# Four-layer graph network on one core: the two input loads of a pair move from SyncE's queue to ScalarE's, and every engine's order of work is drawn again

## What is computed

```
h = relu(layernorm(x)); x = x + deg * (h @ Wi.T + b) + adj @ (h @ Wj.T)          # layer 0
h = relu(layernorm(x)); Wh = h @ W1
    x = x + softmax(mask(leaky(Wh @ a_src [:, None] + Wh @ a_dst [None, :]))) @ Wh  # layer 1
h = relu(layernorm(x)); H = h @ W2          # 128 columns
    x = x + concat(softmax(mask(leaky(H @ a0 [:, None] + H @ a1 [None, :]))) @ H, H)   # layer 2
h = relu(layernorm(x)); q, k, v = h @ Wq.T + bq, h @ Wk.T + bk, h @ Wv.T + bv
    x = x + concat(softmax(mask(q k.T / sqrt(32)), 8 heads) @ v) @ Wo.T + bo        # layer 3
```

## Time and profile before

| | us |
|---|---|
| median of 3 runs | 1317.21 (1314.80 to 1318.49) |
| the profiled execution | 1310.78 |
| its span, first to last instruction | 1309.0 |
| TensorE busy | 1240.0 |
| ScalarE busy | 1074.4 |
| VectorE busy | 1074.3 |
| GpSimd busy | 1011.2 |

### The profile page before, as it was taken

One profiled execution on the slowest core, in us unless ns is written; L12 is line 12 of the kernel. 1 busy time (PEld: TensorE's weight loads), 2 busy tenths in 40 slices (PEclk: granted clock), 3 DMA queues, 4 the chain that ended last, 5 costly groups with the idle time before them and its releaser, 6 DMA issues. The chain is left out here.

```text
span 1309.0 us, 43294 instructions
## 1 busy us (share of the span) xinstructions
PE 1240.0 (95%) x12013; PEld 1106.7 (85%) x12013; DVE 1074.3 (82%) x5137; ACT 1074.4 (82%) x3971; POOL 1011.2 (77%) x1600
## 2 busy tenths in 40 slices
PE   7899999999999999999999999999999999999997
PEld 5788888888888888888888888888888888889986
DVE  5798887888888888888788888888888888888874
ACT  3578888888888888888888888888888888888996
POOL 7778777788787787787787787887887787886763
PEclk9999999999999999999999999999999999999999
DMA  5323342344344434434432433433324434321000
GB/s 143 68 47 43 64 71 52 62 55 70 62 56 69 63 51 71 64 51 67 70 51 63 56 68 63 66 59 62 61 65 62 61 64 62 57 40 22 21 25 34
DMA packets 96523, 77.23 MB, mean 59 GB/s; under 512 B 31264, under 2 KB 88608, under 8 KB 96288
## 3 DMA queue, kind: packets, MB, share of 16 engines
q1 hardware_dynamic: 93808, 72.76, 33.1%
q10 hardware_dynamic: 2480, 1.71, 0.5%
HBM read 57.48 MB, written 16.95 MB: 57 GB/s over the span
## 5 line engine op out<-in xcount | busy, mean ns | idle before, releaser
L891 ACT ACTIVATE exps<-masked,nmax 128x128 f32<-128x128 f32 x1024 | 399.2, 404 | 0.0
L436 POOL TENSOR_TENSOR probs<-exps,rsum 128x512 f32<-128x512 f32 x256 | 266.1, 1040 | 17.7 <-DVE rsum L665 17.4
L657 DVE CUSTOM_DVE_ANT_0 masked<-bank,mask 128x128 f32<-128x128 f32 x1024 | 227.7, 284 | 8.0 <-PE bank L1113 4.3
L407 POOL TENSOR_SCALAR y<-x,nm,rstd 128x256 f32<-128x256 f32 x384 | 209.5, 556 | 11.9 <-issue 11.1
L891 ACT ACTIVATION_READ_ACCUMULATOR exps<-masked,nmax 128x1 f32 x1024 | 208.1, 203 | 0.0
L549 DVE BATCH_NORM_STATS2 stats<-x 128x6 f32<-128x256 f32 x512 | 190.3, 414 | 10.8 <-DMA x<-in_x 8.6
L1002 PE MATMUL bank<-w_hi,ht_hi 128*128 128x258 f32 (+1 forms) x512 | 192.0, 375 | 1.0 <-DVE ht_lo L604 1.0
L614 DVE CUSTOM_DVE_ANT_0 z<-bank,mask 128x128 f32<-128x128 f32 x256 | 64.1, 288 | 151.9 <-ACT bank L860 151.1
L399 POOL TENSOR_TENSOR rstd<-mv,power 128x2 f32<-128x2 f32 x256 | 182.5, 713 | 3.3 <-DVE mv L565 3.3
L371 POOL TENSOR_TENSOR u<-xt,db 128x512 f32<-128x512 f32 x60 | 78.3, 1305 | 134.8 <-issue 134.8
L1004 PE MATMUL bank<-w_hi,ht_lo 128*128 128x258 f32 (+1 forms) x512 | 174.4, 341 | 0.0
(11 more groups left out here) (131 smaller groups left out, 3926.8 us busy)
## 6 DMA issues: line engine op xcount, KB each, us to landing
db<-rows SPq DMA_DIRECT2D x170, 128.0 KB, 5.0
x<-in_x SPq DMA_DIRECT2D x64, 256.0 KB, 4.9
out<-x SPq DMA_DIRECT2D x64, 256.0 KB, 5.4
xt<-in_xt SPq DMA_DIRECT2D x60, 256.0 KB, 5.3
rows<-dst SPq DMA_DIRECT2D x110, 1.0 KB, 3.3
rows<-mv SPq DMA_DIRECT2D x60, 1.0 KB, 3.7
probs<-in_w0t ACTq DMA_DIRECT2D x1, 256.0 KB, 5.6
probs<-in_w0t SPq DMA_DIRECT2D x1, 256.0 KB, 6.6
```

Source lines behind the costliest of these rows:

```text
L407: last = pool.tensor_scalar(y[i][:, b, g], src[:, bx, g], nm[i][:, s, g:g + 1], rstd[i][:, s, g:g + 1], ALU.add, ALU.mult)
L436: pool.tensor_tensor(probs3[:, p % BUFFERS["probs3"], j], exps3[:, p % BUFFERS["exps3"], j], rsum3[:, s, j].unsqueeze(2).to_broadcast([P, ...
L657: last = dve.tensor_tensor_reduce(masked3[:, b, j, i], bank_of(f"sc{j}")[:, i * P:(i + 1) * P], mask[:], scale=-1.0, scalar=-MASKED, op0=A ...
L891: last = act.activation(exps3[:, b, j, i], masked3[:, p % BUFFERS["masked3"], j, i], ACT.Exp, bias=nmax3[:, s, j, i:i + 1], scale=-1.0, ac ...
```

## The change

`load` and `load_transposed` are defined and called in ScalarE's list, with the same waits and semaphores. SyncE keeps the first two loads ahead of its list, the row trips and the stores; on SyncE each row's read now stands right behind its write. All of `LAG`, all bank numbers and the order of every `step(t)` are new. The operations themselves are the same. (`write_mean` and `spread_mean` are also written out on ScalarE, but not called there.)

```
 LAG = {
-       "row_out2": -5, "row_in0": -11, "row_in2": -5, "load_t": -12, "store": 0, "row_out1": -7, "row_out0": -12, "row_in1": -7, "load": -13,
...
+       "row_out0": -7, "row_in0": -7, "row_out2": -1, "row_in2": -1, "row_out1": -3, "row_in1": -3, "store": 4, "p3_3": -1, "rstd1": -6,
...
-    "wh1": (6, "wh1_mm", ('wh1',)),
-    "v": (6, "v_mm", ('v',)),
...
+    "kt": (2, "kt_mm", ('kt',)),
+    "v": (2, "v_mm", ('v',)),
...
+            def load(p):
+                b = p % BUFFERS["x0"]
+                read_before(act, "x0", p, "stats0", "r0")
...
+                act.dma_start(x0[:, b], x_pairs[bass.ds(p, 1)].rearrange("o n g d -> (o n) g d")).then_inc(x_in[b], 16)
...
+            def load_transposed(p):
+                b = (p - ROWS_FIRST) % BUFFERS["xt"]
+                u0_made(act, p - BUFFERS["xt"])
+                act.dma_start(xt[:, b], xt_pairs[bass.ds(p, 1)].rearrange("o q c g n -> (o q) c g n")).then_inc(xt_in[b], 16)
```

More of the change, by code:

```diff
@@ L55 @@
-    "h0t": (0, "h0t", ('h0t_lo',)),
-    "v": (6, "v_mm", ('v',)),
-    "x4b": (2, "x4_mm", ('x4',)),
-    "at2": (3, "e2t", ('at2',)),
-    "kt": (4, "kt_mm", ('kt',)),
-    "h2t": (2, "h2t", ('ht2',)),
-    "x3b": (3, "x3_mm", ('x3',)),
-    "qt": (1, "qt_mm", ('qt',)),
-    "d1": (6, "d1", ('z1',)),
-    "pt1": (4, "pt1", ('p3t_1',)),
-    "hh": (0, "hh_mm", ('hh',)),
-    "sc0": (6, "scores", ('nmax3_0',)),
-    "sc1": (2, "scores", ('nmax3_1',)),
+    "wh1": (4, "wh1_mm", ('wh1',)),
+    "h3t": (5, "h3t", ('h3t_lo',)),
@@ L68 @@
+    "hh": (4, "hh_mm", ('hh',)),
+    "v": (2, "v_mm", ('v',)),
+    "sc0": (1, "scores", ('nmax3_0',)),
+    "sc1": (3, "scores", ('nmax3_1',)),
     "sc2": (5, "scores", ('nmax3_2',)),
-    "sc3": (3, "scores", ('nmax3_3',)),
+    "sc3": (0, "scores", ('nmax3_3',)),
     "zz2": (7, "z2", ('nmax2',)),
-    "m0": (1, "m0", ('mj_lo0', 't0_0')),
-    "ot": (0, "ot_mm", ('ot_lo',)),
-    "at1": (5, "e1t", ('at1',)),
-    "h0": (7, "h0", ('h0t_lo',)),
-    "pt0": (4, "pt0", ('p3t_0',)),
-    "h1t": (6, "h1t", ('h1t_lo',)),
@@ L77 @@
-    "pt2": (5, "pt2", ('p3t_2',)),
-    "x2b": (2, "x2_mm", ('x2',)),
-    "x1b": (0, "s0", ('x1',)),
+    "m0": (6, "m0", ('mj_lo0', 't0_0')),
+    "ot": (4, "ot_mm", ('ot_lo',)),
+    "at1": (0, "e1t", ('at1',)),
+    "pt2": (2, "pt2", ('p3t_2',)),
+    "h1t": (5, "h1t", ('h1t_lo',)),
 }
@@ new lines, in step @@
+                if due(t, "dst1") and not at_an_end(t - LAG["dst1"]):
+                    gather_dst(1, wh, "wh", last_of("wh0", "wh1"), D + 1, t - LAG["dst1"])
+                if due(t, "u0") and t - LAG["u0"] >= ROWS_FIRST:
+                    centre_transposed(t - LAG["u0"])
+                if due(t, "nm2"):
+                    negative_mean(2, "y2", t - LAG["nm2"])
+                if due(t, "rstd2"):
+                    inverse_deviation(2, t - LAG["rstd2"])
+                if due(t, "y2"):
+                    normalise(2, x2, t - LAG["y2"])
@@ L464, in step @@
                 if t == LAG["w3_low2"]:
                     low_w3(2)
-                if due(t, "y3"):
-                    normalise(3, x3, t - LAG["y3"])
-                if due(t, "u0") and t - LAG["u0"] >= ROWS_FIRST:
-                    centre_transposed(t - LAG["u0"])
-                if due(t, "dst1") and not at_an_end(t - LAG["dst1"]):
-                    gather_dst(1, wh, "wh", last_of("wh0", "wh1"), D + 1, t - LAG["dst1"])
-                if due(t, "p3_1"):
-                    normalise_p3(1, t - LAG["p3_1"])
@@ new lines, in step @@
+                if due(t, "rsum1_any"):
+                    inverse_sum(1, "rsum1_any", "x2", t - LAG["rsum1_any"])
+                if due(t, "nmax3_0"):
+                    mask_scores(0, t - LAG["nmax3_0"])
+                if due(t, "t0_0"):
+                    add_own(0, t - LAG["t0_0"])
+                if due(t, "mj_lo0"):
+                    low_mj(0, t - LAG["mj_lo0"])
+                if due(t, "h1t_lo"):
+                    relu_transposed_low(1, ht1_r, last_of("wh0_mm", "wh1_mm"), t - LAG["h1t_lo"])
@@ L686, in step @@
+                if t == LAG["adj_rows"]:
+                    prepare_rows()
+                if due(t, "stats0") and t > LAG["stats0"]:
+                    stats_of(0, x0, t - LAG["stats0"])
+                if due(t, "h3t_lo"):
+                    relu_transposed_low(3, ht3_r, last_of("kt_mm", "qt_mm", "v_mm"), t - LAG["h3t_lo"])
+                if due(t, "nmax2"):
+                    mask_logits(2, mask2, t - LAG["nmax2"])
                 if due(t, "x4"):
                     sum_x4(t - LAG["x4"])
+                if due(t, "rsum3_2"):
+                    inverse_sum3(2, t - LAG["rsum3_2"])
@@ L1148, in step @@
             def step(t):
+                if due(t, "x2_mm"):
+                    attend(1, wh, "wh", D, t - LAG["x2_mm"])
+                if due(t, "s0"):
+                    aggregate(t - LAG["s0"])
+                if due(t, "pt0"):
+                    transpose_p3(0, t - LAG["pt0"])
+                if due(t, "wh0_mm"):
+                    project1(0, t - LAG["wh0_mm"])
+                if due(t, "wh1_mm"):
+                    project1(1, t - LAG["wh1_mm"])
+                if due(t, "h3t"):
+                    transpose_y(3, t - LAG["h3t"])
```

348 lines of the change are left out of this document (167 added, 181 removed), and 22 rows, old and new, of the table LAG.

## The result

The changed kernel takes **1329.41 us** in the median (1325.31 to 1336.48, 6 runs) beside 1317.08 us of the kernel before (1314.80 to 1322.83, 6 runs): 1.0091 times the time, 95% interval 1.0058 to 1.0123. It is slower by 0.9%; the forecast was 1288, in a range of 1266 to 1322. The profiled execution took 1329.42 us.

The account below looks back on a forecast made before the run. The prediction took two DRAM round trips in series on ScalarE's list to bound the kernel, TensorE next at 19.00 us. Terms -43 + 18 - 4 = -29 us gave 1317.2 - 29 = 1288 us, range 1266 to 1322.

Parts of the forecast that it names:

- The ring: ScalarE's list: two DRAM row trips one after the other, 19.72 us, bound the kernel; after the change one trip, 18.2 us.
- The trip of `z2`: From the end of `hh` to `z2` on ScalarE, through layer 2's row in DRAM: 9.04 us, if unchanged.
- The prediction's own sign of being wrong: ScalarE's `z2` beginning over 10.5 us behind `hh` would show the forecast wrong.
- three times 3.63 us: SyncE's standing through the three row writes, within some 13.5 us of 19 occupied; by itself worth nothing.
- The long kind of landing: The mean's row read lands after 6.8 us in the median, 2.1 more than others; `z2`'s read might become so.
- The slower one: Rival, chance 0.17: ScalarE held by its issues (1320 to 1335), or `z2`'s read the long kind (ring 20.3 us, 1345).
- The issues on ScalarE: Issuing two loads between `hh` and `z2`: 0.4 us each, covered by 1.5 us of waiting, no cost.
- The loads' transfers in the rows' way: Rival, chance 0.15: loads on another queue lengthen `z2`'s row read by 1 to 1.5 us; 1300 to 1316 us.
- the term of -43: TensorE: `v_mm` no longer waits for ScalarE's copy `wh`, 0.72 us each in 54 waits; 43 us gained.
- The 18 us for the shorter hop: TensorE waits 0.3 us per pair between `h1t` and `wh1_mm`, over 60 pairs 18 us lost.
- the floor: TensorE's busy time of 19.00 us per pair, taken as the next bound below the ring.
- 0.71 for faster: Summed chance of a faster kernel: 0.50 + 0.13 + 0.08, against 0.10 within and 0.19 slower.

Follow-up runs that it names:

- e3: The kernel before, with both `wh` copies ahead of `z2` on ScalarE: 1342.83 us, 0.9954 of the kernel before.
- e12: The changed kernel with only the mean's read moved behind layer 2's write on SyncE: 1288.57 us, 0.9676 of the kernel before.
- e5: The changed kernel, mean's read behind layer 2's write and mean's write ahead of the store: 1263.18 us, 0.9633 of the kernel before; again 1287.35 us, 0.9648.
- e2: The changed kernel with both loads behind `z2` on ScalarE: 1363.56 us, 1.0100 of the kernel before.
- e9: e5 with both loads behind `z2` on ScalarE: 1281.12 us, 0.9580 of the kernel before.
- e7: e5 with both loads back on SyncE: 1266.60 us, 0.9495 of the kernel before; run again 1268.12 us, 0.9526.
- e4: The kernel before, with both loads moved to ScalarE's list ahead of `z2`: 1359.59 us, 1.0102 of the kernel before.
- e10: The changed kernel with both loads back on SyncE: 1367.08 us, 1.0266 of the kernel before.
- c_after: The changed kernel unedited, profiled on another chip as a control: 1317.45 us, 1.0046 of the kernel before.
- e1: The changed kernel with SyncE's store moved behind the read of layer 2's row: 1355.88 us, 1.0062 of the kernel before.
- e11: The changed kernel storing 16 KB instead of 256 KB per pair, most output unwritten: 1301.19 us, 0.9777 of the kernel before.

## Why the prediction was wrong, point by point

**The ring, right for the changed kernel.** One ring holds only `z2`'s trip now, and I had put the rest of it at 16.64 - 7.5 = 9.1 us; it is 9.02. That the ring of both trips was all that bound the kernel before is not shown: the sum of 19.72 fits, but opening it in the old lists (e3) gained 0.5% where 1 to 3% was expected.

**The trip of `z2`, the step that failed.** The prediction took "9.04 us from the end of `hh` to `z2`, if it lasts as before". It lasted 11.19 in the median, 1.9 more than the 9.25 of before. 1.2 of that is SyncE being late to send the write (1.39 against 0.21), 2.0 the write itself (5.57 against 3.53); the read gave back 0.8, and the copy starts 0.3 earlier (medians, which add up only roughly). The ring is 20.2 instead of 18.2. The prediction's own sign of being wrong, `z2` over 10.5 us behind `hh`, came true.

**SyncE, where it failed.** The prediction counted "three times 3.63 us" of standing and called it "by itself worth nothing". The three waits of the period shown are 7.2, 4.8 and 4.3 us: 16.3 instead of 10.9, and I had priced the mean's write by the row of another write. Worse, I asked only how long SyncE stands, and whether `dst1` finds it free, not what comes due while it stands at the mean's read: `dst2`, the one column on the ring. Both queues stood in full in the section on the change. In the old one the mean's read stands between layer 2's write and its read, where the wait costs nothing; in the new one it stands ahead of the write. e12 moves it back: 0.9676, where the changed kernel stood at 1.0091 and 1.0046.

**The long kind of landing.** "I can't tell why" was said of the mean's read, 6.8 us against 4.7. In the kernel before it was issued 0.4 us behind layer 2's write (604.86):

```profile
605.28 0.37 SPq L280 DMA_DIRECT2D db<-rows  x1
```

In the changed one the two have changed places, and so have the times: the mean's read lands after 4.1 us,

```profile
DMA to landing us min/median/max: 2.8/4.1/6.9
```

and layer 2's write, 0.4 us behind it, takes 5.6. In e5, with the old order, the mean's read is back at 6.9 us, and at 7.2 in its second run. Here whichever goes second is the slow one. A question asked of that row would have priced this.

**The rivals.** The slower one ("ScalarE is held by its own issues or the row trip is the long kind", 0.17) is what happened: 1.6 us more between `hh` and `z2` was its point of decision, 1.9 were measured, and it gave 20.3 us and 1345 where 20.2 and 1329 came out. That is partly luck: it looked for the long kind at `z2`'s read, which got shorter, and it was the write that grew, and SyncE that was late.

**The issues on ScalarE, right.** They last 0.35 to 0.37 us, no activation behind them waits in the changed kernel, and `r0` releases nothing of ScalarE. In e2 and e9 they stand elsewhere and cost 30 us of waiting.

**The loads' transfers in the rows' way** (0.15) was no part of the loss that the runs show. The loads' move by itself has a price all the same. With SyncE's order mended the move costs 1.6% (e5 to e7 in one group, 0.9648 to 0.9495), and 1.0% in the old lists (e4); in another group e7 stands 1.5% under e12, which has the mean's write in another place too. The read to `z2` is 0.4 to 0.5 us longer with the loads on ScalarE, which is the sign of this rival; as the write is shorter, the trips hardly differ. Only behind a mean's read in the wrong place does it help (e10), for there SyncE's queue has no time to spare. The Trainium skill, "DMA: Bandwidth & Descriptors", section "Issuing engines are not separate DMA queues", says that starting DMAs on several engines saves only the sequencer's time; no run here shows a gain from it beyond what SyncE's lateness explains, and e4 and e7 show a cost. The rule of the Trainium skill, same page, section "Queues, rings and completion order", round-robin between the queue rows, could give such a cost; no trace here shows the turns themselves.

**TensorE.** The 0.72 us of `v_mm`'s wait are gone, as the term of -43 had it, but TensorE's idling is not: it now waits for the softmax behind `z2` (L1089). The 18 us for the shorter hop from `h1t` to `wh1_mm` are not there: no TensorE wait for that `h1t_lo` is in the rows of the changed kernel above 2.9 us in all. And the floor was set too high: 19.00 us per pair is what TensorE's busy time came to in a kernel in which it stood 4% idle. In e5 it is 991.53 x 18.80 / 1000 = 18.64 us for the same instructions, where the kernel before had 19.03 on the same chip, both at a clock of 1.00; in e7 again 1226.7 us in the whole against 1240.0, at a mean clock of 0.992 and 0.994. Why is open. With SyncE's order right, the period fell below the 19.4 that I had forecast.

**Chances.** 0.71 for faster rested on a trip that I took over unchanged from a queue whose order was new. The two ends I gave the trip (9.04 and up to 11.1) were both worked out; the weight on the second was too small, for both orders of the queue were there to be compared.

**Open:** why the second of two DMAs of one queue lands 2 to 4 us later, even where the first writes only 1 KB. Nothing here tells a queue's order from the DMA engines' own. How the loss of the changed kernel divides between SyncE's lateness and the slow write is open too, and so is what in e7 is worth 1.6%, when `z2`'s trip is only 0.1 us shorter.

## What to carry to other kernels

Where a queue blocks (a DMA that waits for another to land), read its order as a list of deadlines. For each blocking entry ask which columns or tiles become due behind it while it stands, and put the longest wait inside the trip of the most urgent one, behind its first leg. Price the landing of a DMA by its neighbours in the queue and not by its size alone: rows of the same line with another predecessor are another price. And before moving a transfer to another engine's queue to relieve the first, look at whether the first is late at all; here it was early, and putting the order right (e12, some 4%) was worth more than twice what the move cost (1.6%).

## What the hardware showed that I had not expected

- A 1 KB write to DRAM takes 3.1 to 4.4 us in the median of a run from its issue to the issue of the read that waits for it when nothing was issued in its queue for 2 us or more; 5.1 us in the median when it goes out within 1.2 us behind a 128 KB read (72 cases in the changed kernel, 68 in c_after with 4.9; in other orders of the queue 4.5 in e10 and 7.3 in e1); 7.2 us within 1.2 us behind a 256 KB store (37 and 40 cases, 7.2 in both); 5.1 within 1.2 us behind a 16 KB store (e11, 41 cases).
- A 128 KB read behind a 1 KB write by 0.4 us lands after 6.8 to 7.3 us (before, e5, e7 and their repeats); with nothing issued in its queue in the 2 us before, after 4.0 to 4.9.
- TensorE's busy time for the same 12013 matmuls was 1240.0 us in the kernel before and 1226.7 in e7 again, at nearly the same mean clock (0.994 and 0.992). Its busy time, taken where it waited more, was 1% too high for a floor.
- TensorE's clock fell to 1.2 GHz in the steady stretch where long trips had left it standing for 2 to 4 us: seven times in the changed kernel, six in c_after, never in the kernel before.
- The kernel before took 1310.5 to 1347.3 us in the median over the groups of runs. Its bound is the latency of small DMAs, and most of this difference may be theirs, but no profile of it was taken on the slowest chip, so that stays open.
